# Probabilities of an attention turned half by VectorE blocks and SBUF transfers, scores in fp32 from four row groups

## The reference

```python
x = x + xattn(layernorm(x), ctx, ctx, mask, wq, bq, wk, bk, wv, bv, wo, bo)
#   scores = (q @ k.T) / sqrt(32), masked entries -1e9; probs = softmax(scores); out = (probs @ v) @ wo.T + bo
x = x + ffn(layernorm(x), w_gate, c_fc, c_proj)
#   softmax(x @ w_gate), the two best experts per token, 2048 places per expert, silu(a) * g, c_proj
```

## Time and profile before

| | |
|---|---|
| median of three executions | 3014.14 us |
| profiled execution | 3016.34 us |
| its span, first to last instruction | 3014.5 us |
| mean granted TensorE clock | 0.985 of 2.4 GHz |
| PE busy | 2918.5 us (97%) |
| DVE, ACT, POOL busy | 1532.4, 1551.5, 1258.4 us |
| attention stage | to about 1400 us |

### The profile page before, as it was taken

The page is one execution under the profiler, slowest core; times in us unless marked ns, Lnnn a source line. Parts: engine busy times, 40 slices in busy tenths (PEclk is TensorE's granted clock), DMA queues, the critical chain, the costliest instruction groups (busy, mean ns, idle before and its releaser), DMA issues.

```text
span 3014.5 us, 55229 instructions
## 1 busy us (share of the span) xinstructions
PE 2918.5 (97%) x17696; PEld 2447.6 (81%) x17696; DVE 1532.4 (51%) x5034; ACT 1551.5 (51%) x3942; POOL 1258.4 (42%) x1917
## 2 busy tenths in 40 slices
PE   6999999999999999993999999999999999999998
PEld 6888888888888888872888888888888888888886
DVE  5777777777777777773324233333242332423331
ACT  4788788788788887882323223232232322322321
POOL 4566666676666666663122222121212222222211
PEclk9999999999999999996999999999999999999999
DMA  5444444444444444433434444343434343434322
GB/s 168 118 128 134 130 126 122 125 136 132 125 118 136 128 133 126 125 97 115 111 78 98 81 96 83 90 92 89 89 92 95 83 92 77 98 81 95 69 43 28
DMA packets 290774, 315.34 MB, mean 105 GB/s; under 512 B 46912, under 2 KB 235328, under 8 KB 288960
## 3 DMA queue, kind: packets, MB, share of 16 engines
q1 hardware_dynamic: 227424, 178.48, 22.4%
q0 software_dynamic: 32768, 67.26, 12.7%
q10 hardware_dynamic: 30304, 66.07, 6.6%
HBM read 109.53 MB, written 67.90 MB: 59 GB/s over the span
## 4 chain that ended last, share of the span: by engine, by line
PE 52%; DMA 1%; SPq 0%; issue 0%; POOL 0%; DVE 0%; ACT 0%; POOLq 0%
PE a_ps L1248 17%; PE g_ps L1248 17%; PE y_ps L1263 17%; DMA out<-y,recs 0%; SPq L1041 0%; DMA xg<-xn_rows,gather_ids 0%; POOL xg L1087 0%; DMA lists<-table 0%; DMA x_quarters<-xg 0%; DVE xe_lo L1182 0%; POOL out L1115 0%; ACT xe_hi L1142 0%; DVE x_turned L1195 0%; ACT y L1175 0%; DVE act_part L1195 0%
## 5 line engine op out<-in xcount | busy, mean ns | idle before, releaser
L1115 POOL DMA_INDIRECT out<-y,recs x128 | 206.7, 1615 | 1185.8 <-ACT y L1175 860.4
L389 POOL TENSOR_SCALAR probs<-probs,row_inv 128x256 f32<-128x256 f32 x1024 | 486.4, 486 | 405.9 <-DVE row_inv L606 392.7
L597 DVE CUSTOM_DVE_ANT_0 probs<-scores_ps,mask_add,row_any 128x256 f32<-128x256 f32 x1024 | 454.5, 480 | 266.3 <-PE scores_ps L813 247.3
L497 ACT ACTIVATE probs<-probs,low 128x256 f32<-128x256 f32 x1024 | 514.3, 505 | 115.0 <-DVE low L597 103.2
L1222 DVE TENSOR_TENSOR hidden<-act_part,g_ps 128x512 f32<-128x512 f32 x192 | 132.0, 688 | 860.8 <-ACT act_part L1161 857.4
L478 ACT COPY probs_t<-probs_t_ps 128x512 f32<-128x512 f32 x512 | 298.9, 584 | 149.7 <-PE probs_t_ps L825 79.2
L1248 PE MATMUL a_ps<-xe_hi,fc_hi 128*128 128x512 f32 x768 | 300.4, 391 | 40.1 <-DVE xe_lo L1182 39.9
L825 PE MATMUL probs_t_ps<-ident,probs 128*128 128x128 f32 x2048 | 311.3, 274 | 7.6 <-POOL probs L389 7.6
L1248 PE MATMUL a_ps<-xe_hi,fc_lo 128*128 128x512 f32 x768 | 299.8, 390 | 0.0
L1248 PE MATMUL a_ps<-xe_lo,fc_hi 128*128 128x512 f32 x768 | 299.7, 390 | 0.0
L1161 ACT ACTIVATE act_part<-a_ps 128x512 f32<-128x512 f32 x192 | 114.8, 598 | 359.0 <-PE g_ps L1248 355.6
(11 more groups left out here) (173 smaller groups left out, 6600.6 us busy)
## 6 DMA issues: line engine op xcount, KB each, us to landing
k_stack<-qk_hi SPq DMA_DIRECT2D x512, 64.0 KB, 2.1
q_stack<-qk_hi SPq DMA_DIRECT2D x512, 64.0 KB, 2.7
x_quarters<-xg SPq DMA_DIRECT2D x512, 64.0 KB
fc_raw<-in_c_fc SPq DMA_DIRECT2D x24, 1024.0 KB, 5.7
k_stack<-qk_lo SPq DMA_DIRECT2D x256, 64.0 KB, 2.1
q_stack<-qk_lo SPq DMA_DIRECT2D x256, 64.0 KB, 3.0
out<-x_xn ACTq DMA_DIRECT2D x32, 512.0 KB, 3.4
xn_rows<-x_xn ACTq DMA_DIRECT2D x32, 512.0 KB, 3.5
```

The costliest lines, as they stand in the source:

```text
L389: last = nc.gpsimd.tensor_scalar(probs[:, r, t, :], probs[:, r, t, :], row_inv[:, r, t:t + 1], 1.0, ALU.mult, ALU.mult)
L497: last = nc.scalar.activation(probs[:, s % 4, t, :], probs[:, s % 4, t, :], ACT.Exp, scale=-1.0, bias=low[:, s % 4, t:t + 1], accum_out=ro ...
L597: last = nc.vector.tensor_tensor_reduce(out=probs[:, s % 4, t, :], in0=scores_ps[s % 2][:, t, :], in1=mask_add[:, t, :], scale=row_any[:, ...
L1115: nc.gpsimd.indirect_dma_start(out=out[:, :], out_offset=bass.IndirectOffsetOnAxis(ap=recs[:, i * CT + t, 0:1].bitcast(U32), axis=0), in_= ...
```

## The change

The expert block stays as it is. In `attention_block`:

- **Scores.** `stacks` and its 48 transfers, and the high and low parts of q and k, are gone. ACT writes q and k of a batch in fp32 into `qk` (two batches deep); PE makes the scores of a chunk of four heads in one go, each head with K = 32 in its own row group of the array and into its own bank, `scores_ps[r]` for r = 0 to 3.
- **Even chunks** of four heads are turned by DVE in 32x32 blocks (`turn`, four instructions of 128x512 a chunk, each waits for all four heads to be scaled) into `blocks`, and SP moves the blocks between partitions into `probs_m` (`move`, 16 transfers of 64 KB a chunk). **Odd chunks** are turned by PE as before, but into the chunk's own scores banks (`probs_turn`), and copied by ACT (`turned_out`).
- **Order.** The slots are replaced by phases, one a chunk. The step now reaches over five batches: projections of n+1, heads of n, outputs and second layer norm of n-1, gate and places of n-2, records of n-3; steps go to 34. `probs` is a ring of 8 heads instead of 4. The values' projection of batch n moves from step n-1 into step n.
- Everything that went through bank a to c has new places among them; the two attention groups of a pair of chunks stand next to each other.

```diff
-        stacks = [sb(f"{name}_stack", [len(PASSES) * DK, DC, HPC, SEQ], F32R) for name in "qk"]
+        qk = sb("qk", [P, 2, 2, DC, SEQ])
+        probs = sb("probs", [P, RING, TILES, SEQ])
+        blocks = sb("blocks", [P, GROUPS, HPC * TILES * TILES * DK])
+        probs_m = sb("probs_m", [P, GROUPS, HPC * TILES * TILES * DK])
+        probs_t = sb("probs_t", [P, HPC, TILES, SEQ])
...
+                def move(g):
+                    need(sp, attended, g - 1)
...
+                    for a in range(GROUPS):
+                        settle(sp)
+                        sp.wait_ge(turned, g // 2 * GROUPS + a + 1)
+                        for j in range(GROUPS):
+                            sp.dma_start(probs_m[a * DK:(a + 1) * DK, j, :],
+                                         blocks[j * DK:(j + 1) * DK, a, :]).then_inc(moved, 16)
...
+                def turn(g, a):
+                    dve.wait_ge(normed, (g + 1) * HPC)
+                    if a == 0:
+                        need(dve, moved, QUARTERED * (g // 2))
...
+                    nc.vector.transpose(blocks[:, a, :].rearrange("p (b l) -> p b l", l=DK),
+                                        of[:, :, a, :]).then_inc(turned, 1)
...
+                def score(g):
+                    b, c = divmod(g, DC)
+                    pe.wait_ge(q_ready, g + 1)
+                    pe.wait_ge(k_ready, g + 1)
+                    need(pe, masked, g * HPC)
+                    if g % 2:
+                        need(pe, pe_copied, g // 2 * HPC)
+                    for t in range(TILES):
+                        for r in range(HPC):
+                            rows_of = slice(r * DK, (r + 1) * DK)
+                            last = nc.tensor.matmul(scores_ps[r][:, t, :], qk[rows_of, b % 2, 0, c, t * P:(t + 1) * P],
+                                                    qk[rows_of, b % 2, 1, c, :], start=True, stop=True)
+                    last.then_inc(scored, 1)
...
+                def probs_turn(g, r):
+                    if r == 0:
+                        pe.wait_ge(normed, (g + 1) * HPC)
+                    if g + 1 < BATCH * DC:
+                        pe.wait_ge(masked, (g + 1) * HPC + r + 1)
+                    for u in range(TILES):
+                        for t in range(TILES):
+                            last = nc.tensor.transpose(scores_ps[r][:, u, t * P:(t + 1) * P],
+                                                       probs[:, (g * HPC + r) % RING, t, u * P:(u + 1) * P],
+                                                       ident[:, :])
+                    last.then_inc(pe_turned, 1)
```

More of the change, by code:

```diff
@@ L321, in _ @@
+                for g in range(0, BATCH * DC, 2):
+                    move(g)
                 sp.wait_ge(defaults_stored, 16 * (EXPERTS + 2))
@@ L546, in _ @@
+                for n in STEPS:
+                    step(n)
             @block.vector
@@ L743, in step @@
+                def step(n):
+                    heads, proj, tail, late = has(n), has(n + 1), has(n - 1), has(n - 2)
+                    if n == -2:
+                        moments_x(0)
+                        normalise_x(0)
+                        for t in range(TILES):
+                            x_lo(0, t)
                         split_w(0)
@@ L756, in step, with scores @@
                         dve.wait_ge(pool_const, 11)
-                    if is_step(n, -2):
                         split_w(1)
-                steps(dve, step)
+                    def scores(g):
+                        for r in range(HPC):
+                            mask_scores(g * HPC + r)
+                            if r >= 2:
+                                invert(g * HPC + r - 2)
+                    g = n * DC
+                    if heads:
+                        scores(g)
+                    if proj and n >= 0:
+                        moments_x(n + 1)
@@ new lines, in step @@
+                    if heads:
+                        invert(g * HPC + 2)
+                    if has(n - 3):
+                        record(n - 3)
+                    if heads:
+                        invert(g * HPC + 3)
+                    if proj and n >= 0:
+                        normalise_x(n + 1)
+                    if n == 0:
+                        split_w(3)
+                    if heads:
+                        for a in range(GROUPS):
+                            turn(g, a)
+                        scores(g + 1)
@@ new lines, in step @@
+                    if late:
+                        logits_out(n - 2)
+                    if tail:
+                        attn_lo(g - 2)
+                        attn_lo(g - 1)
+                    if heads:
+                        invert(g * HPC + HPC + 2)
+                    if proj and n >= 0:
+                        x_lo(n + 1, 0)
+                    if heads:
+                        invert(g * HPC + HPC + 3)
+                    if heads:
+                        scores(g + 2)
+                    if proj and n >= 0:
+                        x_lo(n + 1, 1)
@@ new lines, in step @@
+                    if tail:
+                        x2_out(n - 1, 0)
+                    if heads:
+                        invert(g * HPC + 2 * HPC + 2)
+                    if late:
+                        route(n - 2)
+                    if heads:
+                        invert(g * HPC + 2 * HPC + 3)
+                    if tail:
+                        x2_out(n - 1, 1)
+                    if heads:
+                        for a in range(GROUPS):
+                            turn(g + 2, a)
+                        scores(g + 3)
@@ L781, in columns, with rows @@
                     return last
[L783 to L786 removed]
+                def rows(bank, matrix, lhs, t, done, half, split=None, base=0):
+                    chunks = range(half * DC // HALVES, (half + 1) * DC // HALVES)
+                    first = half == 0
                     for c in chunks:
@@ new lines, in gate @@
+                def gate(b):
+                    if b == 0:
+                        pe.wait_ge(setup_loaded, 80)
+                        pe.wait_ge(dve_const, 6)
+                    pe.wait_ge(x2t_ready, (b + 1) * TILES)
+                    for c in range(DC):
+                        last = nc.tensor.matmul(bank_a[c * DK:(c + 1) * DK, 0:SEQ], wg[:, c, :],
+                                                x2t[:, c, :], start=True, stop=True)
+                    last.then_inc(gate_full, 1)
```

1084 lines of the change are left out of this document (560 added, 524 removed).

## The result

The changed kernel took 3001.04 us (median of 5 runs, 2996.49 to 3001.97), the kernel before 3015.28 us beside it: a ratio of 0.9947, 95% interval 0.9935 to 0.9958. So it is faster by half a per cent, where the prediction said 3031 us and slower; the time lies inside the range. The profiled execution took 2996.49 us, its span is 2994.7 us.

The account below looks back on a forecast made before the run. PE bounded the kernel before; afterwards a DVE, ACT and POOL loop would, at 42.15 us a batch against 41.53. +21 us over 32 batches plus the ends made +17: 3033 profiled, 3031 median, range 2965 to 3095.

Parts of the forecast that it names:

- The bound: Attention stage: PE, full before, would stop being the bound, about 187 us busy per 200.
- each wait named: PE waits at the probs turns for POOL or DVE, at x_turn for the logits copy, at scores for q_ready.
- The loop: Per-batch chain of score, mask, exp, scale and transposes across engines: 42.15 us against 41.53, +0.65 a batch, +21 in 32.
- the ends: First and last steps: scores 10 us earlier, short steps saving less (+2.4), drain +4.
- M1 to M2: Start of DVE's first-chunk masks to second-chunk masks: 12.2 us, through exp, record, scale and turns; PE's scores tie.
- M2 to M3: Second-chunk masks to third-chunk masks: 8.5 us, x_turn waiting for the logits copy behind four masks, then keys and score.
- M3 to M4: Third-chunk masks to fourth-chunk masks: 11.7 us, through exp 11, scale and block transposes.
- M4 to M1': Fourth-chunk masks to the next step's first masks: 9.7 us, second layer norm queued before them, costing 2.4.
- part of the way, 40 to 41.3, 2970 to 3008: Shorter handoffs or layer norm not holding the masks: step 40 to 41.3 us, total 2970 to 3008; chance 0.17.
- (b): Row-group scores: weight loads queue, 1.76 us for 1.05 a chunk, +1.9 a step, 3091 us; chance 0.13.
- (c): Row-group scores do not overlap at all: PE alone 48.7 us a batch, 3245 us; chance 0.03.
- The reading of 32-element runs at nothing: Attention reading probs_m in runs of 32 elements: taken as 0 extra PE time, at most +2.0 us.

Follow-up runs that it names:

- c_after: The changed kernel unedited, run as a control in another launch beside the kernel before: 3185.42 us, ratio 1.0568.
- f1_records_interleaved: Changed kernel with the four record transfers issued one behind each head's scale of head group 1 instead of in a row: 3094.68 us, ratio 1.0263.
- after: The changed kernel itself, unedited, as first timed and profiled: 3001.04 us, ratio 0.9947 to the kernel before.
- g2_again: Changed kernel with record transfers spread, second layer norm's root before head 14's scale, logits copy between two masks; repeated in another launch: 2927.03 us, ratio 0.9703.
- g3_spread_no_turns: Changed kernel with record transfers spread and DVE's block transposes and their SBUF moves left out: 2965.67 us, ratio 0.9831.

## Why the prediction was right or wrong

**The bound: right.** PE ceased to be it; 187 us busy of 200 were forecast and measured, and each wait named stands where it was put (the one for q_ready is short, 0.2 us a step).

**The loop: mechanism right, size wrong.** This is the step that failed: the sum of the loop, forecast at 42.15 us, +0.65 a batch against before, measured 40.65 (40.93 with the falls of the clock), 0.57 under before. Over 32 batches that is -18 us where +21 was forecast, 39 us apart, and it turned the sign; the ends, below, took back 2 of them (3033 forecast for the profiled execution, 2996.5 measured).

| term | forecast | measured | what the trace shows |
|---|---|---|---|
| M1 to M2 | 12.2 | 11.97 | record() took 1.8 us (611.33 to 613.13) for 2.5, so the reciprocal of head 3 followed ACT at M1+7.9 and not at 8.4; the scale took back 0.3 (1.27 for 0.94) |
| M2 to M3 | 8.5 | 8.36 | the four masks and the logits' copy, done 0.3 earlier |
| M3 to M4 | 11.7 | 11.24 | reciprocal and scale at once behind exp 11, transposes at +8.8 for 9.2 |
| M4 to M1' | 9.7 | 9.08 | head 14's scale done at +6.9 for 7.3; normalise to first mask 1.02 for 1.2 |

Each is a little less, and the sign of the result hung on 0.65 of 42. The prediction's own rival "part of the way, 40 to 41.3, 2970 to 3008", for shorter handoffs, with its 0.17, is what came. That the time lies inside the stated range is that rival's doing, not the forecast's.

**Rivals (b) and (c): fell.** The row-group scores are 16 issues in 1.15 us, the next operation 1.07 behind their start. Their loads last 0.185 us each, 16 x 0.185 = 2.96 us in line; they ran abreast. So the Trainium skill's Part 3 of TensorE: Matmul & The Clock Gate, by which row groups overlap, decided, and not its LDWEIGHTS cost added up. The forecast's 1.4 us a chunk was 0.33 too much, 1.3 a batch of PE's sum, which hid behind the loop.

**The reading of 32-element runs at nothing: right**: the 16 issues on moved data take 0.86 us to the next group's start (614.12 to 614.98), those on PE's own 0.98 to the scores behind them. The moves held 0.5 us in all, once.

**Ends: near in sum, wrong in a piece.** The first scores came at 31.15 (35 said), but the second chunk's at 44.81: step 0 was not shortened, since it waits 3.98 us for the values' weights. In sum the ends give -1.4 us (-19.8 less 32 x -0.57) where -3.6 was forecast.

**What was missing: the records.** The prediction has no term for POOL's indirect transfers of the records in their new place. In the launch that was timed first they cost nothing; in three of the four controls they cost 155 to 187 us against the undisturbed time. That the first time lay within the range owes something to luck: in those three launches the kernel is 61 to 90 us above the upper end of 3095. The rows of before showed no late update, but its trace had the sign, updates up to 1.2 us late beside single transfers 2.2 us apart. A DMA that moves has to be counted with its spacing and with what stands beside it.

## What to carry to other kernels

Where a chain of handoffs is within 2% of the old period, its sign is not known: give it even odds, and look instead for the waits in it that an order alone can remove (here 2.04 and 0.68 us a batch, worth 74.5 us). Read an edit's gain in its own term of the loop in the trace; that held here even where the whole time was disturbed. Don't issue GpSimd's indirect transfers in a row beside work whose semaphores are on the critical loop; put them singly where engines have slack, POOL's own next work included. Run the unchanged kernel as a control in every launch: four edits were judged by a fault that none of them had brought.

## What the runs showed of the hardware

While GpSimd issued four indirect transfers back to back (1.3 us apart), TensorE's semaphore updates of the scores reached the others 1.8 to 4.6 us late in four of six launches, though the matmuls ran on; in the other two they were not late at all, at the same distance between the same instructions. With two in a row they were 0.4 to 1.5 us late, beside single ones in the kernel before up to 1.2 us. Updates of the other engines were not late in these traces.

Waits of TensorE of some 4 us once a step went with 125 us at the 1.2 GHz level in 17 steps (c_after), waits of 2.4 us with 79 us in 18 steps (f1_records_interleaved), waits of up to 2 us with four stretches of 3.4 us in 20 steps (after), and with TensorE busy 196.8 of 200 us (g2_again), or 760 of 800 (g3_spread_no_turns), there was none from 300 to 1100 us.
